# Message products of a graph layer on quarters of the TensorE array, with a new order of the step

## What is computed

```python
h = silu(edge_scalars @ (Wfc1 / sqrt(16)));  w = h @ (Wfc2 / sqrt(64))      # 192 weights per edge
f0 = x0 @ Wl1_0 * a * inv8;  f1 = einsum('num,uv->nvm', x1, Wl1_1) * a * inv32
e0, e1 = f0[edge_src], f1[edge_src]
mid0 = w0 * e0 * sh0;                 mid1 = w3 * einsum('eum,em->eu', e1, sh1) / sqrt(3)
mid2 = w1 * e0 * sh1 (by component);  mid3 = w2 * e1 * sh0
n0..n3 = means of mid0..mid3 over the edges of each destination
scal, vec = concat(n0, n1), concat(n2, n3)
conv = concat(scal @ Wl2_s, vec @ Wl2_v) * a * inv96;  alpha = scal @ Wa * a * inv96
out = layernorm(x + sc(x) + alpha * conv)          # sc: a linear map of x, scaled by a
```

## Time and profile before

| | |
|---|---|
| median of 3 runs | 905.8 us (902.68 to 907.19) |
| profiled execution, its own time | 905.83 us |
| its span, first to last instruction | 903.9 us |
| busy in the span: TensorE, VectorE, ScalarE, POOL | 95%, 90%, 70%, 79% |
| mean granted TensorE clock | 0.992 |

### The profile page before, as it was taken

How to read it: one execution, slowest core, us unless ns; L and a number is a source line. 1 busy time by engine, 2 the same in 40 slices (tenths; PEclk the granted TensorE clock), 3 DMA queues, 4 the chain that set the end, 5 groups by cost and what they waited for, 6 DMA issues and landing times.

```text
span 903.9 us, 32652 instructions
## 1 busy us (share of the span) xinstructions
PE 855.1 (95%) x10688; PEld 726.4 (80%) x10688; DVE 810.6 (90%) x2797; ACT 630.4 (70%) x1961; POOL 715.3 (79%) x804
## 2 busy tenths in 40 slices
PE   2999999999998999999999988999999999999994
PEld 1788787788887877888888877888888888888884
DVE  3788999999996999999999987999999999999997
ACT  1555555555554655565565554999999999999997
POOL 6777777777776776777777712999999999999994
PEclk9999999999998999999999999999999999999998
DMA  6455544455456666567764413899999999999973
GB/s 183 121 166 165 167 137 130 133 131 143 131 135 129 187 204 190 164 172 203 208 181 132 134 64 120 249 308 314 315 318 326 310 315 312 321 304 318 319 258 146
DMA packets 87539, 186.77 MB, mean 207 GB/s; under 512 B 17646, under 2 KB 48138, under 8 KB 87371
## 3 DMA queue, kind: packets, MB, share of 16 engines
q1 hardware_dynamic: 50715, 93.00, 32.0%
q0 software_dynamic: 18944, 35.81, 18.1%
q10 hardware_dynamic: 17712, 55.87, 17.9%
HBM read 119.66 MB, written 64.95 MB: 204 GB/s over the span
## 4 chain that ended last, share of the span: by engine, by line
PE 70%; DVE 12%; issue 9%; POOL 5%; DMA 3%; ACT 1%; DVEq 0%; ACTq 0%; POOLq 0%
PE ps L831 20%; PE ps L772 7%; PE ps L847 7%; PE ps L751 6%; PE ps L817 6%; POOL gat L620 5%; PE ps L849 5%; PE ps L769 4%; PE ps L732 4%; PE ps L738 4%; DVE mid L1021 3%; DMA gat<-spread,srcs 3%; PE ps L714 3%; DVE z L1039 3%; PE ps L712 2%
## 5 line engine op out<-in xcount | busy, mean ns | idle before, releaser
L620 POOL DMA_INDIRECT gat<-turned,srcs x196 | 190.6, 973 | 68.9 <-issue 61.7
L620 POOL DMA_INDIRECT gat<-spread,srcs x196 | 189.5, 967 | 61.8 <-issue 59.1
L898 ACT ACTIVATE te<-ps 128x512 f32<-128x512 f32 x196 | 106.4, 594 | 124.8 <-PE ps L738 124.8
L831 PE MATMUL ps<-win,eas 60*128 60x162 f32 x2352 | 189.0, 306 | 0.7 <-DVE eas L1364 0.7
L772 PE MATMUL ps<-wy,mid 128*128 128x161 f32 x784 | 182.4, 314 | 0.0
L831 PEld LDWEIGHTS ps<-win,eas 60*128 60x128 f32 x2352 | 164.9, 186 | 17.0 <-issue 10.5
L686 POOL TENSOR_TENSOR gat<-eas,gat 128x640 f32<-128x640 f32 x98 | 152.4, 1555 | 15.2 <-ACT eas L943 12.3
L1045 DVE SCALAR_TENSOR_TENSOR msg<-ps,sha,z 128x161 f32<-128x161 f32 x392 | 151.0, 385 | 13.9
L769 PE MATMUL ps<-wy,mid 128*128 128x97 f32 x784 | 141.6, 262 | 0.2 <-DVE mid L1021 0.2
L1021 DVE TENSOR_TENSOR mid<-ps,te 128x512 f32<-128x512 f32 x196 | 133.1, 680 | 3.2 <-PE ps L751 3.2
L921 ACT ACTIVATE te<-gat,shift,rstd 128x160 f32<-128x160 f32 x292 | 131.2, 527 | 1.4 <-DVE shift L1311 1.3
(11 more groups left out here) (108 smaller groups left out, 1515.1 us busy)
## 6 DMA issues: line engine op xcount, KB each, us to landing
win<-rows SPq DMA_DIRECT2D x392, 114.6 KB, 4.1
rows<-msg SPq DMA_DIRECT2D x98, 326.0 KB
out<-te ACTq DMA_DIRECT2D x47, 640.0 KB, 6.2
xin<-x_g ACTq DMA_DIRECT2D x76, 322.0 KB, 5.1
kept_x<-x_g SPq DMA_DIRECT2D x16, 322.0 KB
gat<-turned,srcs POOLq DMA_INDIRECT x196
gat<-spread,srcs POOLq DMA_INDIRECT x196
eas<-ea_t SPq DMA_DIRECT2D x7, 384.0 KB, 4.7
```

The lines of the kernel that those rows point to most:

```text
L620: pool.indirect_dma_start(out=gat[:, slot, first:first + of.shape[1]], out_offset=None, in_=of, in_offset=bass.IndirectOffsetOnAxis(ap=src ...
L831: last = nc.tensor.matmul(agg_ps[b1][:, 2 * h + k, 0:SW], hot[side(h), b1, k, c, :], win[side(h), (RING * i + b - 1) % WIN_RING, k, c, 0:S ...
L898: nc.scalar.activation(e_sb[:, t, :], e_ps[:, t], ACT.Copy).then_inc(e_out[t], 1)
```

## The change

A message row gets five chunks of 33 columns (165 instead of 163): each of 32 features and one more for the count, the label, the gate or nothing. The order of features in all tables follows. In `combine`, each pair's four products with full weights become 16 products on 64x64 quarters of the array, which put chunks on both sides of the border between two PSUM banks; products of the lower 64 rows write ahead of the border, those of the upper 64 rows behind it. ScalarE then copies the scalar chunks of both tiles at once, and VectorE makes the vector chunks of both tiles with two instructions (three components: two and one) and one sum per tile. TensorE's order in a step was first layer, transposes and products by pair, e, w; it becomes transposes of both pairs, products of both pairs, w, first layer, e. ScalarE copies both transposes, then both pairs' chunks, then the first layer, then e; VectorE makes both halves of `mid` first, then label and both finishes. In the second stage the window sums have 164 columns, and ScalarE's scaled copies read five runs of 32 columns.

```diff
-GATE, CNT, LABEL = 0, 1 + D, 2 + D
-SW = 2 + D
-AW = 3 + D
+CHUNK = MUL1 + 1
+CHUNKS = 5
+AW = CHUNKS * CHUNK
+SW = AW - 1
+M_A, M_C, M_S, M_B = 0, CHUNK, 2 * CHUNK, 4 * CHUNK
+CNT, LABEL, GATE = M_A + MUL1, M_C + MUL1, M_S + MUL1
 RCNT, GRA = SW, SW + 1
 LAB, RSTD = GRA + 1, GRA + 1 + 6
 HALF = 64
@@ -77,9 +82,8 @@
-Y_A = MUL1
-Y_C = Y_A + 1 + D
-YW = Y_C + 1 + MUL0
+LANES = 2 * CHUNK
+YB = 4 * LANES
...
-        y_ps = [ps[:, n:n + 2, 0:YW] for n in (2, 6)]
-        heads_ps = ps[:, 6:8, YW:YW + T // 2]
-        wrong_ps = ps[0:1, 6, YW + T // 2:YW + T // 2 + 1]
+        heads_ps = ps[:, 6:8, 0:T // 2]
+        wrong_ps = ps[0:1, 6, T // 2:T // 2 + 1]
+        def y_at(k, t, j, count=1, every=1):
+            flat = ps[:, (2, 6)[k]:(2, 6)[k] + 2, :].rearrange("p c e -> p (c e)")
+            lanes = flat[:, 512 - YB:512 + YB].rearrange("p (j t w) -> p j t w", t=2, w=CHUNK)
+            return lanes[:, j + 4:j + 4 + (count - 1) * every + 1:every, t, :]
...
             def first_layer(q):
-                if q >= 1:
-                    pe.wait_ge(h_out, 2 * q)
-                    pe.wait_ge(t_out, 2 * q)
+                pe.wait_ge(t_out, 2 * q + 2)
...
+                    last = nc.tensor.matmul(h_ps[:, k], wt[half, w:w + P], eas[half, q // 2, :],
+                                            start=True, stop=True)
+                last.then_inc(h_ready, 1)
...
             def turn(q, k):
                 pe.wait_ge(q_ready, q + 1)
+                if q >= 1:
+                    pe.wait_ge(h_out, 2 * q)
...
             def combine(q, k):
-                p, y = 2 * q + k, y_ps[k]
+                p = 2 * q + k
                 if p == 1:
                     pe.wait_ge(heads_out, 2)
+                if p == 0:
+                    pe.wait_ge(wy_ready, 12)
                 for t in range(2):
-                    if p == 0:
-                        pe.wait_ge(wy_ready, 12)
                     pe.wait_ge(mid_ready[t], q + 1)
                     if k == 0:
                         pe.wait_ge(e_out[t], min(q + 2, NS))
                     if q >= 1:
                         pe.wait_ge(msg_ready[t], p - 1)
-                    nc.tensor.matmul(y[:, t, 0:W_Y1 - W_YA], mid[:, q % 2, t, 0, k, :],
-                                     wy[:, 0:W_Y1 - W_YA], start=True, stop=True)
-                    of = (W_Y1, W_Y1B)[t] - W_YA
-                    nc.tensor.matmul(y[:, t, W_Y1 - W_YA:YW], mid[:, q % 2, t, 1, k, :],
-                                     wy[:, of:of + VEC + 1 + MUL0],
-                                     start=True, stop=True).then_inc(y_ready[t], 1)
+                low, high = slice(0, HALF), slice(HALF, P)
+                made = ((0, 0, low, W_V, y_at(k, 0, -4)[:, :, 0:MUL1]),
+                        (0, 0, high, W_YA, y_at(k, 0, 1, 2)),
+                        (0, 1, low, W_Y1, y_at(k, 0, -3, 3)),
+                        (0, 1, high, W_Y1, y_at(k, 0, 0, 2, 3)),
+                        (1, 0, low, W_YA, y_at(k, 1, -2, 2)),
+                        (1, 0, high, W_V, y_at(k, 1, 3)[:, :, 0:MUL1]),
+                        (1, 1, low, W_Y1B, y_at(k, 1, -4, 2)),
+                        (1, 1, high, W_Y1B, y_at(k, 1, 0, 3)))
+                for t, c, half, w, y in made:
+                    width = y.shape[1] * y.shape[2]
+                    for edges in (low, high):
+                        last = nc.tensor.matmul(
+                            y[edges], mid[half, q % 2, t, c, k, edges],
+                            wy[half, w - W_YA:w - W_YA + width].rearrange(
+                                "p (j w) -> p j w", j=y.shape[1]), start=True, stop=True)
+                last.then_inc(y_ready, 1)
             def step(d):
-                if alive(d, 0):
-                    first_layer(d)
                 for k in range(2):
                     if alive(d, 0):
                         turn(d, k)
+                for k in range(2):
                     if alive(d, 3):
                         combine(d - 3, k)
                 if alive(d, 1):
-                    weigh(d - 1)
+                    find_w(d - 1)
+                if alive(d, 0):
+                    first_layer(d)
+                if alive(d, 1):
+                    find_e(d - 1)
...
             def take_turned(q, k):
-                p, b = 2 * q + k, q % 2
-                act.wait_ge(t_ready, p + 1)
+                b = q % 2
+                act.wait_ge(t_ready, 2 * q + k + 1)
+                if q >= 2:
+                    act.wait_ge(e_ready, q - 1)
+                nc.scalar.activation(t_sb[:, b, :, k, :], t_ps[:, k], ACT.Copy).then_inc(t_out, 1)
+            def take_first(q):
+                b = q % 2
+                act.wait_ge(h_ready, q + 1)
                 if q >= 2:
                     act.wait_ge(w_ready, q - 1)
-                    act.wait_ge(e_ready, q - 1)
-                nc.scalar.activation(h_sb[:, b, k, :], h_ps[:, k], ACT.Silu,
-                                     scale=FC_IN ** -0.5).then_inc(h_out, 1)
-                nc.scalar.activation(t_sb[:, b, :, k, :], t_ps[:, k], ACT.Copy).then_inc(t_out, 1)
+                for k in range(2):
+                    nc.scalar.activation(h_sb[:, b, k, :], h_ps[:, k], ACT.Silu,
+                                         scale=FC_IN ** -0.5).then_inc(h_out, 1)
             def take_second(q, k):
                 p = 2 * q + k
-                for t in range(2):
-                    act.wait_ge(y_ready[t], p + 1)
-                    if p >= 2:
+                act.wait_ge(y_ready, p + 1)
+                if p >= 2:
+                    for t in range(2):
                         act.wait_ge(msg_ready[t], p - 1)
-                    nc.scalar.activation(z[:, k, t, 0:1 + MUL0], y_ps[k][:, t, Y_C:YW],
-                                         ACT.Copy).then_inc(zc_ready[t], 1)
+                flat = ps[:, (2, 6)[k]:(2, 6)[k] + 2, :].rearrange("p c e -> p (c e)")
+                first, other = 512 - 3 * LANES, 512 + LANES + CHUNK
+                c = flat[:, first:first + 2 * (other - first)].rearrange(
+                    "p (t w) -> p t w", t=2)[:, :, 0:2 * LANES].rearrange(
+                    "p t (j w) -> p t j w", j=2)[:, :, :, 0:CHUNK]
+                nc.scalar.activation(
+                    z[:, k, :, M_S:M_B].rearrange("p t (j w) -> p t j w", j=2), c,
+                    ACT.Copy).then_inc(zc_ready, 1)
             def step(d):
                 for k in range(2):
                     if alive(d, 0):
                         take_turned(d, k)
+                for k in range(2):
                     if alive(d, 3):
                         take_second(d - 3, k)
+                if alive(d, 0):
+                    take_first(d)
...
-                        last = nc.scalar.activation(agg[:, b0, k, :], agg_ps[b0][:, k, 1:1 + D],
-                                                    ACT.Copy, scale=coef[:, b0, k:k + 1])
+                        last = nc.scalar.activation(
+                            agg[:, b0, k, :].rearrange("p (j w) -> p j w", w=MUL1),
+                            agg_ps[b0][:, k, 0:AW].rearrange(
+                                "p (j w) -> p j w", w=CHUNK)[:, :, 0:MUL1],
...
             def label(q):
-                half = slice(q % 2 * QUAD, (q % 2 + 1) * QUAD)
-                if q >= 2:
+                if q >= 1:
+                    for t in range(2):
+                        dve.wait_ge(msg_ready[t], 2 * q)
+                nc.vector.tensor_copy(
+                    z[:, :, :, LABEL],
+                    dsts[:, QUAD * q:QUAD * (q + 1)].rearrange("p (k t) -> p k t", t=2)
+                ).then_inc(label_ready, 1)
+            def finish(q, k):
+                p, ring = 2 * q + k, q % SHA_RING
+                pair = slice(2 * k, 2 * k + 2)
+                flat = ps[:, (2, 6)[k]:(2, 6)[k] + 2, :].rearrange("p c e -> p (c e)")
+                first, other = 512 - 4 * LANES, 512 + 3 * LANES + CHUNK
+                v = flat[:, first:first + other - first + MUL1]
+                dve.wait_ge(zc_ready, p + 1)
+                if p >= 2:
+                    for t in range(2):
+                        dve.wait_ge(msg_ready[t], p - 1)
+                spread = sha[:, ring, pair, :].rearrange("p t m -> p (t m)")
+                nc.vector.tensor_tensor(
+                    z[:, k, :, M_A:M_S].rearrange("p t (j w) -> p t j w", j=2)[:, :, :, 0:MUL1],
+                    two_of(v, other - first, MUL1).unsqueeze(2).broadcast_to([P, 2, 2, MUL1]),
+                    two_of(spread[:, 1:], 5, 2).unsqueeze(3).broadcast_to([P, 2, 2, MUL1]),
+                    ALU.mult).then_inc(zb_ready, 1)
+                nc.vector.tensor_tensor(
+                    z[:, k, :, M_B:M_B + MUL1],
+                    two_of(v, other - first, MUL1),
+                    two_of(spread[:, 3:], 2, 1).broadcast_to([P, 2, MUL1]),
+                    ALU.mult).then_inc(zb_ready, 1)
+                if k == 0 and q >= 2:
```

(49 more changed lines are left out.)

129 lines of the change are left out of this document (70 added, 59 removed).

## The result

The changed kernel takes 925.8 us (median of 4 runs, 921.5 to 929.0), the kernel before 904.2 (901.6 to 907.2): a ratio of 1.024 (95% interval 1.0215 to 1.027), slower. The forecast was 887. The profiled execution took 928.08, with a span of 926.3.

A forecast was written before the change was run, and what follows sets the result against it. Gathers at 5.0 us per step were to bind the first stage: last gather 508, first-stage end 532.5, plus second stage 352.7, a span of 885.2 us and a time of 887; range 877 to 906.

The forecast's parts named there:

- The loop through the shared banks: First stage: e's copy, first pair's products, chunk copies, VectorE's finish, then e again; claimed 4.6 us a step.
- TensorE's own arm: First stage, TensorE's own sequence in that loop: 1.2 + 1.07 + 1.06 + 0.22 + 1.0 = 4.6 us.
- the gathers: First stage, POOL: four gathers at 1.25 us need 5.0 us per step and bind after the change; chance 0.62.
- TensorE (5.22): First stage before the change: TensorE's step of 5.22 us, within 5% of POOL (5.0) and VectorE (4.98).
- TensorE at 85%: First stage, sign that the prediction is right: TensorE busy near 85%, pausing before e.
- The products: First stage, TensorE: 16 products on quarters per pair; a step's products fall from 2.2 to 1.07 us.
- No concurrency: Rival: quarters run only two at a time, products 2.0 us, loop 5.5, total 935 us; chance 0.04.
- VectorE's reads: Rival: reads of several runs over two banks cost VectorE more, 935 us; chance 0.15 shared with ScalarE's second-stage copies.
- VectorE at 4.72: First stage: VectorE's own work per step falls from 4.98 to 4.72 us, a pair costing 1.05.
- the 21 us: First stage: waits and long issues of gathers beyond 499 us; 9 kept, last gather ending at 508.
- The second stage: After the last message: 164 columns instead of 162 add 2.2 us, giving 352.7; ScalarE's copies add nothing.
- a rival that I had sought in the steps: Rival that pauses lower TensorE's clock: 4.2 us of work becomes 7 or 8, 200 us over the stage; chance 0.02.

The follow-up runs named there:

- the order alone with alternating banks: Kernel before with the new order on all engines and old products, e's banks alternating between steps: 908.0 us, ratio 1.001, step 5.10.
- the order alone: Kernel before with the new order on all engines but the old products and old chunks: 915.8 us, ratio 1.012, step 5.30.
- alternating banks: Changed kernel, e in banks 2, 3 in even steps and 6, 7 in odd ones, pair whose banks e's copy does not hold first: 899.7 us, ratio 0.993.
- the quarters alone: Changed kernel with quarter products, 33-column chunks and 165-wide rows, but the old order on all engines: 928.1 us, ratio 1.025, step 5.42.
- Wider rows alone: Kernel before with message rows of 165 numbers instead of 163, two of them zeros that nothing reads: 903.4 us, ratio 0.999.
- the kernel before with alternating banks: Kernel before, only e's banks alternating between steps and the pair whose banks e does not need first: 906.0 us, ratio 1.001, step 5.22.

## Why the prediction was wrong

**The step that failed is "The loop through the shared banks", 4.6 us.** It measured 5.32. (Its own terms, 2.4, 1.1 and 1.0, add to 4.5.) Its first part was right: it has the first pair's chunks copied 2.4 us from its zero, and they are, counted from the start of e's copy (402.11 to 404.53, 2.42). That was luck in part: the products started at 1.34 and not 1.2, and ScalarE's copy of the chunks waited for them (0.29 in its row) and not for the copies of the transposes. Three terms behind that were too small. e was put at 1.0, the distance of starts on TensorE; from its start until ScalarE can start the copy it takes 1.36. The restart of TensorE behind VectorE's last sum was put at nothing; it takes 0.25. A pair's finish, from the end of the chunks' copy to the last sum, was put at 1.1; it takes 1.29 (404.53 to 405.82), mostly because the first sum starts 0.13 behind the multiply that it needs (404.78 + 0.22 to 405.13), where 0.04 had been taken, and because the last sum was counted by its distance of starts (0.30) and not to its end (0.39). That is 0.36 + 0.25 + 0.19, and 0.02 in the first part: 0.82, from 4.5 to 5.32. "TensorE's own arm", put at 4.6 too, comes to 5.15 (1.34 + 1.20 + 0.97 + 0.28 + 1.36), by the same term for e above all; both are over the 5.0 of the gathers, which were to bind. The rows of before showed the first two: e starts at 306.39 and its copy at 307.73, 1.34; and the first pair's last sum of that step stands there so, in order of time on VectorE of the kernel before:

```profile
305.75 0.39 DVE L1045 SCALAR_TENSOR_TENSOR msg<-ps,sha,z 128x161 f32<-128x161 f32 x1
```

It ends at 306.14, and e starts at 306.39, 0.25 later. I had taken distances of starts for the time in which a result is ready.

**The kernel before was already on such a ring.** "TensorE (5.22)" was taken as work, and only "less work on TensorE alone" was to be worth 0.2 us a step. Its ring in the old order is e 1.13, w 0.86, first layer 0.32, transposes 0.38, products to sums 2.28 (303.86 to 306.14) and restart 0.25: 5.22. In all 91 steps read in this way e starts 0.25 or 0.26 behind the end of VectorE's sums, while its distance from the start of TensorE's last product goes from 0.29 to 3.4: it is the sums that release it. With the same products in another order a step takes 5.10 (the order alone with alternating banks), so about 0.12 us of the usual step of before was waiting, if the order itself costs nothing. In the usual step none of that shows as idle time; in 24 steps of the kernel before it does, and it was TensorE's largest wait (total us, times, longest):

```profile
PE ps L732 <- DVE msg L1045: 14.0, 24, 3.1
```

The Trainium skill (Perfetto Trace Analysis, Tensor Engine Instruction (MATMUL, LD_WEIGHTS)) says that the end of a matmul in a trace is estimated and not observed; the trace agrees so far as that wait is hidden under the row of the last product. A busy share of 97.4% was no proof of work, then: the order alone shows TensorE 100% busy from 300 to 400 us at 5.30 a step, and 99.6% at 5.10 once the banks alternate.

**Why less work made it slower.** The quarters took their time out of the products, which stand inside the wait for the first pair's finish or right ahead of it; the first pair has to be made whole before ScalarE copies its chunks, 0.82 behind the start of its products (307.24 to 308.06) where the first tile's chunks were copied 0.75 behind before, so products to sums went from 2.28 to 2.38, and the transposes ahead from 0.38 to 0.48. TensorE gained only idle time. The new order moved w and the first layer into that wait, which opens this ring, but it put e last, so that e's copy stands bare ahead of the products: the other ring, 5.32. Opened by alternating banks, the same change is worth having: 4.91 a step, 899.7 us against 908.0 for the old products in the same order; in the two profiles 5.5 us of it lie in the first stage (544.1 against 549.5).

**Right.** TensorE at 85% (86%), by luck: 4.2 us of a 5.0 us step were meant, and 86% of 5.3 to 5.4 is 4.6. The products: 1.07 forecast, 1.20 to the next line's start, so the quarters do work side by side; "No concurrency" falls. "VectorE's reads" falls too, though its time of 935 was the nearest: a sum of 165 in five runs takes 385 ns, as one of 161 did (group means of lines 1118 and 1045); the prediction's argument against it, that today's small multiply lies on the line, showed nothing, since that multiply is one of the two points the line was drawn through.

**Not right, and hidden by the ring.** The next bound was to be the gathers at 5.0 with VectorE at 4.72 behind them. With the rings open VectorE takes 4.91, most of the 0.19 in its two finishes (2.27 for 2.1), and it sets the steps from 300 us on. The last gather ends at 515.7 there and not at 508: some 17 of the 21 us stay, where 9 were kept.

**The second stage** was forecast 2.2 us longer and is 9.1. The columns are right: the usual group takes 3.465 us for 3.448, 1.7 us in all. 1.6 are the first group, 5.03 for 3.45: the granted clock was 0.50 ahead of it, a rival that I had sought in the steps and not at the end of the stage. The rest, 5.7, are eight late groups, where I had written of "transfers that TensorE does not wait for"; that the DMA share stood at 1.00 from 600 to 700 us was passed over, and whether it matters here is not shown. Who waited, 575 to 900 us (total us, times, longest):

```profile
DVE ps L1431 <- DMA win<-rows: 14.7, 15, 2.0
...
SPq L484 <- PE ps L869: 4.2, 7, 0.8
```

In this stretch SP hands out the windows' loads nearly back to back: it waits 4.2 us for TensorE, while with the quarters alone, which have the same rows and no late group, it is ahead and waits 27.7 us. Wider rows alone made none late, the order alone with the narrow rows had 4 late groups in one profile and 14 in another, and the changed kernel had 8 and 3. All eight profiles with the new order on ScalarE have some; of the others, the kernel before with alternating banks has two, and the rest none but next to a first group at a low clock. Why that order should slow SP's queue in a later stage is not shown and stays open: of the 22 us between the two profiles, these 5.7 have no cause named.

## What to carry to other kernels

Ahead of taking work off a busy engine, follow one result around a whole step and add the times until it is ready, not the distances of starts: if that ring is as long as the step, shorter work becomes idle time. A buffer that two users share in turns closes such a ring, and an in-order engine closes a second one through its own program; opening one shows the other, so both have to be opened before the smaller work pays. To find which arm binds, shorten one thing that lies on one arm alone and see whether the step moves.

## What the runs showed of the hardware

TensorE started 0.25 us after the end of the row that released it, behind ScalarE (403.20 to 403.45; in other steps up to 0.42) and behind VectorE (405.82 to 406.07; in 89 of 90 steps the same within 0.01); VectorE started 0.04 after ScalarE (404.53 to 404.57). In the last steps of the first stage, with TensorE busy 2.43 of 5 us, the granted clock was 0.80 in that stretch and 0.50, which is 1.2 of 2.4 GHz, in the next, and the first 24 window sums of the second stage took 3.50 us instead of 1.93; in the kernel before, where TensorE was busy 4.77 and 2.88 of the last two stretches of 5 us, it stayed at 1.00. Reading five runs over two banks cost VectorE nothing that 392 sums could show (385 ns for 165 columns, as for 161 before).
